# Order of the causal mask and the output tail in a pipelined linear-attention loop

## The reference, cut to what matters

```python
def _phi(x, omega):
    proj = jnp.einsum('bhsd,md->bhsm', x, omega)
    z = proj - 0.5 * jnp.sum(x * x, axis=-1, keepdims=True)
    z = z - jnp.max(z, axis=-1, keepdims=True)
    return jnp.exp(z) / jnp.sqrt(m) + FEAT_EPS

def step(carry, qkv):                       # scan over the 2048 positions
    S_kv, s_k = carry
    S_kv = S_kv + kt[..., :, None] * vt[..., None, :]
    s_k = s_k + kt
    num = jnp.einsum('bhm,bhmd->bhd', qt, S_kv)
    den = jnp.einsum('bhm,bhm->bh', qt, s_k)
    return ((S_kv, s_k), num / (den[..., None] + FEAT_EPS))
```

## Time and profile before

| | |
|---|---|
| median of 8 runs | 2491.01 us |
| lowest run | 2488.79 us |
| profiled execution | 2491.65 us |
| its span (slowest core) | 2490.1 us |
| spans of the 8 cores | 2468.9 to 2490.1 us |
| TensorE busy | 1932.8 us (78%) |
| VectorE busy | 762.5 us (31%) |
| ScalarE busy | 612.4 us (25%) |
| GpSimd busy | 67.4 us (3%) |

### The profile page before, as it was taken

One profiled execution on the slowest core, in us unless ns is written; L12 is line 12 of the kernel. 1 busy time (PEld: TensorE's weight loads), 2 busy tenths in 40 slices (PEclk: granted clock), 3 DMA queues, 4 the chain that ended last, 5 costly groups with the idle time before them and its releaser, 6 DMA issues.

```text
span 2490.1 us, 31179 instructions; the slowest of 8 cores (2468.9 to 2490.1 us)
## 1 busy us (share of the span) xinstructions
PE 1932.8 (78%) x10312; PEld 952.8 (38%) x10480; DVE 762.5 (31%) x1701; ACT 612.4 (25%) x1414; POOL 67.4 (3%) x111
## 2 busy tenths in 40 slices
PE   1999959997132788875473599999996799969999
PEld 1444424443111455543231244444443444424444
DVE  5211211113200277776436422222224311101111
ACT  6211111111000278776326300000003411001100
POOL 1000010000000000000000000000001000000000
PEclk9999979998566899985596799999998899989999
DMA  9973063411999300000100233333335251163431
GB/s 220 119 104 102 1 101 51 102 51 19 112 118 120 64 19 19 19 2 1 34 1 1 85 138 133 136 135 136 135 135 106 47 102 51 52 99 54 102 135 51
DMA packets 81753, 199.89 MB, mean 80 GB/s; under 512 B 3776, under 2 KB 49088, under 8 KB 73408
## 3 DMA queue, kind: packets, MB, share of 16 engines
q0 software_dynamic: 42032, 82.38, 23.8%
q1 hardware_dynamic: 37264, 107.11, 12.5%
q10 hardware_dynamic: 2304, 8.39, 0.9%
HBM read 271.86 MB, written 37.75 MB: 124 GB/s over the span
## 4 chain that ended last, share of the span: by engine, by line
PE 66%; DMA 11%; another core or an unknown queue 6%; ACT 6%; DVE 6%; issue 4%; POOL 0%; DVEq 0%; ACTq 0%; SPq 0%; POOLq 0%
PE p L410 13%; PE p L390 13%; PE p L1163 9%; PE p L1131 9%; PE p L472 5%; PE p L466 4%; PE p L631 3%; DMA BufC<-Wq_bf 2%; DMA BufC<-Wk_bf 2%; DMA BufC<-Wv_bf 2%; DMA BufC<-wuT_i 2%; PE p6a L762 2%; DMA x_tm<-xin 1%; DVE amT L845 1%
## 5 line engine op out<-in xcount | busy, mean ns | idle before, releaser
L390 PE MATMUL p<-fmA,BufC 128*128 128x512 bf16 x1504 | 364.7, 382 | 52.0 <-DMA BufC<-wuT_i 50.0
L410 PE MATMUL p<-fmA,BufC 128*128 128x512 bf16 x1506 | 362.0, 381 | 1.6
L426 DVE SCALAR_TENSOR_TENSOR actB<-p,tmpF 128x512 bf16<-128x512 f32 x192 | 132.8, 692 | 589.9 <-PE p L410 578.0
L472 PE MATMUL p<-BufC,actB 128*128 128x512 bf16 x768 | 292.1, 380 | 3.9 <-DMA BufC<-wdT_bf 2.1
L466 PE MATMUL p<-BufC,actB 128*128 128x512 bf16 x736 | 279.7, 380 | 13.7 <-DMA BufC<-wdT_bf 9.5
L421 ACT ACTIVATE tmpF<-p 128x512 f32<-128x512 f32 x192 | 114.7, 598 | 647.3 <-PE p L390 647.3
L390 PEld LDWEIGHTS p<-fmA,BufC 128*128 128x128 bf16 x1536 | 150.7, 98 | 235.1 <-issue 57.3
L1163 PE MATMUL p<-actB,BufC 128*128 128x512 bf16 x1001 | 224.2, 379 | 5.7 <-DVE actB L1141 4.6
L1131 PE MATMUL p<-fmA,BufC 128*128 128x512 bf16 x1003 | 221.6, 380 | 9.1 <-DMA BufC<-W_bf 8.0
L410 PEld LDWEIGHTS p<-fmA,BufC 128*128 128x128 bf16 x1536 | 151.0, 98 | 183.3 <-issue 3.6
L631 PE MATMUL p<-fmA,BufC 128*128 128x512 bf16 x490 | 125.7, 398 | 115.4 <-DMA BufC<-Wq_bf 70.3
(11 more groups left out here) (110 smaller groups left out, 1763.9 us busy)
## 6 DMA issues: line engine op xcount, KB each, us to landing
BufC<-W_bf SPq DMA_DIRECT2D x64, 1024.0 KB, 5.2
BufC<-wgT_i POOLq DMA_DIRECT2D x32, 768.0 KB, 17.0
BufC<-wuT_i POOLq DMA_DIRECT2D x32, 768.0 KB, 20.5
W_bf<-W_sw POOLq DMA_DIRECT2D x2, 8192.0 KB, 139.3
BufC<-wdT_bf SPq DMA_DIRECT2D x4, 3072.0 KB, 12.2
BufC<-wdT_bf SPq DMA_DIRECT2D x12, 1024.0 KB, 10.1
wdT_bf<-wdT_i POOLq DMA_DIRECT2D x1, 6144.0 KB, 121.0
x_tm<-xin ACTq DMA_DIRECT2D x8, 512.0 KB, 21.2
```

The source lines that it names most:

```text
L390: e.matmul(pg[pi][:, 0:512], BufC[:, wg_off + k * 768 + hcl * 128: wg_off + k * 768 + (hcl + 1) * 128], fmA[:, k * 2048 + tt0 + tsl * 512: ...
L410: e.matmul(pu[pi][:, 0:512], BufC[:, wu_off + k * 768 + hcl * 128: wu_off + k * 768 + (hcl + 1) * 128], fmA[:, k * 2048 + tt0 + tsl * 512: ...
L426: e.scalar_tensor_tensor(actB[:, hc * 1024 + tsl * 512: hc * 1024 + (tsl + 1) * 512], pu[pi][:, 0:512], INV127, tmpF[:, pi * 512:(pi + 1) ...
L472: e.matmul(db[:, 0:512], actB[:, hc * 1024 + tl * 128: hc * 1024 + (tl + 1) * 128], BufC[:, hc * 1024 + 512: hc * 1024 + 1024], start=(hc ...
```

## The change

The tail of unit sl-8 is emitted behind the mask of unit sl-7 and no longer ahead of it. On VectorE the mask becomes the first instruction of the slot; the order on the other engines is the same, and so are the instructions and what each of them waits for.

```diff
             for sl in range(NE + 9):
                 if 0 <= sl - 8 < NE:
                     st_o(sl - 8)
-                    st_tail(sl - 8)
                 if 0 <= sl - 7 < NE:
                     st_mask(sl - 7)
+                if 0 <= sl - 8 < NE:
+                    st_tail(sl - 8)
                 gq = sl // 32 + 1
                 adv_gen(gq)
```

## The result

The changed kernel took 2445.87 us in the median of 11 runs; the kernel before, run beside it again, 2493.73. The ratio is 0.9816, with a 95% interval of 0.9807 to 0.9826, or 45.8 us off 2491.0. The forecast was 2442 with a range of 2435 to 2458.

What follows compares the result with a forecast made beforehand. No engine was full; a loop through several engines, with the mask paid in every bare slot, set the pace. Gains of 31.4 (bare) + 14.9 (V) + 2.5 (last six) = 48.8 us gave 2442 us, range 2435 to 2458.

Steps and rivals of the forecast that it cites:

- bare slot: Attention-loop slot from 96 on, without the eight matmuls; forecast from 3.13 to 2.15 us, saving 31.4 us over 32.
- V slots: 48 loop slots with eight 256-column matmuls (L666); only those without a VectorE cast gain, 14.9 us in three runs.
- loop (a): In a bare slot: tail, accumulate (L808/L805), matmuls from L776 to the next L885; put at 2.02 us.
- (b): In a bare slot: VectorE's own instructions, start to start; 2.06 us, claimed to become the bound.
- signs by which the prediction was to be called wrong: QK slots move, V slots' clock below 1.00, VectorE idles ahead of L885 in bare slots, or a later stage lengthens.
- QK slots: 48 loop slots with eight 512-column matmuls (L631); forecast to gain nothing.
- p4 loop: In QK slots: matmuls L631, ScalarE's evacuation of p4, next matmuls; 2.73 us, claimed to cover the mask.
- last six slots: Slots 129 to 134, 2.5 us each, without projections; forecast gain 2.5 us in all, between 0 and 3.6.
- Rival 1: Tied loops don't overlap, mask to `st_o` stays whole: bare and even V slots at 2.40, 2461 us; chance 0.15.
- Rival 2: TensorE's clock comes back in bare slots, VectorE's 2.06 + 0.04 holds: 2440 us; chance 0.17.
- Rival 3: No change: the wait on the mask in the loop really stands for something else; 2491 us, chance 0.03.
- Rival 4: Slower: in QK slots the mask waits for L821 and holds the tail; 2508 to 2535 us, chance 0.02.

Runs made afterwards that it cites:

- e3: Changed kernel with L821 again made to wait for the tail of its slot: ratio 0.9918 to the kernel before, 2470.6 us.
- e5: Changed kernel with the tail emitted last in every slot on VectorE, behind L721: ratio 0.9938 to the kernel before.
- e9: Changed kernel with TensorE's two projections issued ahead of L776, VectorE's order untouched: ratio 0.9782 to the kernel before.
- e6b: Changed kernel without L746 (scaling and epsilon of the features), run a second time for its trace: ratio 0.9783 to the kernel before.
- e8: Changed kernel with seven instead of eight matmuls L631 in each group: ratio 0.9766 to the kernel before, 2432.7 us.

## Why the prediction was right, and where a term was off

The mechanism. The mask was paid in every bare slot because it stood behind a tail that waited for `st_o`, with L821 behind the mask. Shown by e3: with the order changed and the wait for the tail put back, a bare slot takes 2.80 and about half of the gain is gone. In the changed kernel L821's wait for the mask is 5.2 us. That VectorE then becomes the bound, at 2.06, came true in the V slots and not in the bare ones.

The bare slots. Forecast 2.15, measured 2.26 in most slots and 73.7/32 = 2.30 in the mean, 26.6 us gained, not 31.4. The term that was mis-sized is loop (a), put at 2.02: it is 0.77 + 0.44 + 1.04 = 2.25. Most of the error is one part, L776 to the next L885, put at 0.87. That number was read from a chain, in which a piece begins only where the piece before it ends; the transposes L762 and L776 overlap, so that the chain gives L776 only what is left behind the transposes' modelled end, at 1123.64. The timeline of the same slot of the kernel before has its true start:

```profile
1123.43 0.32 PE L776 MATMUL p<-actB,BufC 128*128 128x65 bf16 x2
...
1124.51 0.16 DVE L885 TENSOR_SCALAR den_t<-p6b 128x2 f32<-128x2 f32 x1 [0.93 <-PE p6b L875]
```

That is 1.08 us from start to start, and 1.07 in the median of the bare slots before. In the sum of 3.09, which holds L762 as well, the short piece did no harm; in loop (a), which holds L776 without L762, it made the loop too short by 0.2, and with 1.08 the prediction's own sum would have been 0.73 + 0.28 + 0.14 + 1.08 = 2.23. The two other parts grew by 0.04 (L885 to L808 0.77, not 0.73) and 0.02 (L808 to L776 0.44, not 0.42). So loop (a) was the bound and not VectorE, (b). e5 and e9 cut this loop in two different places and the slots went to 2.06 and 2.11; e6b took work from VectorE and they didn't move. What I had allowed for loops that hold one another, 0.05, had the right sign and was no substitute for that reading. Two of the signs by which the prediction was to be called wrong thus showed, small: VectorE waits 0.14 us ahead of L885 in bare slots, and the QK runs moved by 2.5 us in all. VectorE is busy 87% of the time there, not 90%.

The V slots. Forecast 4.80 for a pair, and in the changed kernel most pairs are 2.11 + 2.70 = 4.81, with VectorE in one unbroken row:

```profile
1000.32 0.15 DVE L885 TENSOR_SCALAR den_t<-p6b 128x2 f32<-128x2 f32 x1
...
1001.50 0.69 DVE L681 CAST actB<-p 128x512 bf16<-128x512 f32 x1
1002.10 0.68 DVE L721 TENSOR_REDUCE st_nm<-p 128x4 f32<-128x512 f32 x1
...
1003.03 0.15 DVE L885 TENSOR_SCALAR den_t<-p6b 128x2 f32<-128x2 f32 x1
...
1005.14 0.15 DVE L885 TENSOR_SCALAR den_t<-p6b 128x2 f32<-128x2 f32 x1
```

L885 to L885 is 2.71 with the cast and 2.11 without it, and no idle time is listed. The forecast run of 38.4 measured 39.3: what is missing is in the slots at the ends of a run (2.34 for slots 17 and 31) and in single pauses of 0.1 to 0.25 us, whose cause wasn't tried. VectorE's own row is also 2.11 in this order, not 2.06, above all because L899 is now followed by L808, 0.24 behind it, where the mask followed 0.20 behind. e6b shows the bound, in the slots without a cast.

The QK slots. Forecast: nothing, as the p4 loop covers all. Within a run that holds (2.72 to 2.73 a slot before and after, and e8 moved them by what it took from that loop). But the first slots of a run aren't in that loop yet: slots 33 and 34 took 2.99 and 3.02 before and 2.10 and 2.67 after. Such first slots gave most of the 2.5 us of the two runs, which I hadn't counted. The 1.3 us of the first nine slots is the mask's own earlier place in its slot and no gain. The last six slots gave 3.9, over my upper bound of 3.6, which had put 1.93 on each of them, with ScalarE's row, though the last ones have no exponentials.

The rivals. Rival 1 (bare slots 2.40) was wrong in its path, but a bare slot came out between it and the forecast; the worth of naming it was the upper end of the range. Rival 2: the granted clock in bare slots stayed at 0.50. The rule of the Trainium skill (TensorE: Matmul & The Clock Gate, Part 1: The HAM clock gate), that activity releases the throttle, didn't show here, with TensorE busy 81% of those slots by the profile's count; no run here shows what would have released it. By e5 and e9, in which VectorE's row of 2.06 to 2.11 holds the bare slots, a shorter loop (a) would have given some 5 to 7 us. Rival 3 falls by the result. Rival 4, the mask as a plug ahead of the tail in QK slots, came closer than the time tells. A QK slot of the changed kernel:

```profile
934.46 0.68 DVE L721 TENSOR_REDUCE st_nm<-p 128x4 f32<-128x512 f32 x1
...
934.99 0.28 PE L821 MATMUL p<-BufC 128*128 128x128 bf16 x2
...
935.44 0.42 DVE L845 TENSOR_TENSOR amT<-p,maskji_s 128x256 bf16<-128x256 f32 x1 [0.30 <-PE p L821]
...
935.70 0.19 PE L875 MATMUL p6b<-sbT,BufC 128*128 128x65 bf16 x1
...
936.00 0.16 DVE L885 TENSOR_SCALAR den_t<-p6b 128x2 f32<-128x2 f32 x1
```

L721 ends at 935.14 and L821 at 935.27, 0.13 later, as in most QK slots; the limit that I gave was 0.15. The mask waits 0.30 us for it, the tail follows at 936.00, 0.11 behind the end of L875 (935.89), as before the change: it isn't held. e5 shows the same danger with another plug: the tail stood behind a cast that had to wait for the matmuls, L885 began at 1002.47 though the last matmul of its `st_o` had ended by 999.7, and the three V runs took 36 us more than in the changed kernel, where the change gives them 11.9. VectorE's queue, which the Trainium skill (TensorE: Matmul & The Clock Gate, Architectural detail: the array is 16× 32×32, not 1× 128×128) calls strictly first in, first out, behaved so there.

Sum: -11.9 - 26.6 - 3.9 - 2.5 - 1.3 = -46.2 against -48.8, or -45.1 between points that don't move. Terms too large by 7.8 us and terms forgotten or too small by some 4 set each other off in part. That the total is closer than its parts is luck.

## What to carry to other kernels

In a pipeline written out by hand, put on each engine first what has its inputs from the slot before, and behind it what must wait for this slot; but look at the kinds of slot apart, for an instruction that waits in one kind (the cast) makes the same order costly there, and the best order can differ from slot to slot. When a wait on one engine is removed, work out the loop that is left from starts in the timeline, not from pieces of a chain: where instructions overlap, a chain cuts the later one short, and a loop that holds only that one comes out too short, here by 0.2 us of 2.25. And measure a gain between instructions that the change doesn't move. A cut of each candidate loop at a place of its own, as in e5, e9 and e6b, tells the bound from a neighbour 0.15 us away, which the time of the whole kernel could hardly do.

## What was new about the hardware

A TensorE sequence behind a wait cost no restart that these traces show. The same instructions (L776, two projections, four matmuls of L866 and L875, at the granted clock of 0.50) took 1.07 us from the first start to the start of L885 when they followed the transposes without a pause (median of the bare slots before), and 1.04 when they began after a wait for VectorE. VectorE's instructions overlap as well: the next one started 0.60 us behind a row maximum of 0.68, and 0.33 behind a mask of 0.42. So a wait can be there where no idle time is listed: the 0.14 us ahead of L885 in most bare slots stands in no line of the waits. And TensorE stayed at 0.50 through some 70 us of bare slots (1094 to 1164 us) in which the profile counts it busy 81% of the time on the profiled core; the granted clock was 0.50 in that stretch on all eight cores.
